# A fused attention and feed-forward kernel: both first maxima and both first exponentials of two units taken at once

## What is computed

```
x = x + tanh(g_xattn) * attention(layernorm(x), ctx)
x = x + tanh(g_ffn)   * ffn(layernorm(x))

attention, per batch and head h:
  scores = q_r[h] @ k_r[h].T          # 512 x 1024, inner size 64
  attn   = softmax(scores)            # row maximum, exponential with row sum, division
  ctx_c  = attn @ kv_rope             # 512 x 128
  out   += ctx_c @ (w_kc_kv[h].T @ Wo[h])
ffn: act_quant(rmsnorm(.)) @ w1, @ w2; silu(a) * b; act_quant(rmsnorm(.)) @ w3
```

## Time and profile before

| | |
|---|---|
| median of 3 runs | 731.63 us |
| the profiled execution, its own time | 732.04 us |
| its span (first to last instruction) | 730.2 us |
| outside the span | 1.84 us |
| busy: PE, DVE, ACT, POOL | 98%, 78%, 67%, 35% |
| PE's granted clock | full speed in all 40 slices |
| pair 7, turns of unit 0 begin | 562.72 us |
| pair 7, turns of unit 2 begin | 596.77 us |

### The profile page before, as it was taken

The page is one execution under the profiler, slowest core; times in us unless marked ns, Lnnn a source line. Parts: engine busy times, 40 slices in busy tenths (PEclk is TensorE's granted clock), DMA queues, the critical chain, the costliest instruction groups (busy, mean ns, idle before and its releaser), DMA issues.

```text
span 730.2 us, 11950 instructions
## 1 busy us (share of the span) xinstructions
PE 715.8 (98%) x4142; PEld 531.6 (73%) x4142; DVE 569.0 (78%) x1016; ACT 487.0 (67%) x821; POOL 252.5 (35%) x235
## 2 busy tenths in 40 slices
PE   9899999999999999999999999999999999999997
PEld 8577788777877787778777877787777676645553
DVE  6778867777787777767878787878887889999873
ACT  3677666666666656666666666666676766478876
POOL 4744422222212222222222222222322334677651
PEclk9999999999999999999999999999999999999999
DMA  7401164114010401040114113543250101000001
GB/s 278 151 31 58 39 236 169 34 39 149 29 57 29 158 29 57 29 158 31 59 58 157 59 59 123 174 153 114 70 188 11 29 1 58 1 1 26 19 30 44
DMA packets 22124, 58.32 MB, mean 80 GB/s; under 512 B 4032, under 2 KB 7232, under 8 KB 21312
## 3 DMA queue, kind: packets, MB, share of 16 engines
q1 hardware_dynamic: 19904, 44.96, 18.3%
q0 software_dynamic: 784, 10.49, 3.8%
q10 hardware_dynamic: 1392, 2.29, 0.9%
HBM read 51.45 MB, written 6.29 MB: 79 GB/s over the span
## 4 chain that ended last, share of the span: by engine, by line
PE 83%; DVE 7%; ACT 3%; POOL 3%; issue 2%; DMA 2%; ACTq 0%; SPq 0%; POOLq 0%; DVEq 0%
PE ps_b L1377 14%; PE ps_s L1324 13%; PE ps_ctx L1335 9%; PE ps_ctx L1337 7%; PE ps_ctx L1336 7%; PE ps_s L587 4%; PE ps_b L1233 4%; PE ps_b L1231 4%; PE ps_b L1232 4%; PE ps_b L1297 2%; PE ps_b L638 2%; PE ps_b L1266 2%; PE ps_b L1299 2%; PE ps_b L1298 2%; PE ps_b L1303 2%
## 5 line engine op out<-in xcount | busy, mean ns | idle before, releaser
L1128 POOL TENSOR_SCALAR E<-E,small 128x1024 f32<-128x1024 f32 x128 | 148.1, 1157 | 415.1 <-DVE small L1680 415.1
L1471 ACT ACTIVATE et_hi<-ps_b 128x512 fp32r<-128x512 f32 x256 | 152.8, 602 | 163.9 <-PE ps_b L1377 163.7
L1636 DVE TENSOR_TENSOR et_lo<-ps_b,et_hi 128x512 fp32r<-128x512 f32 x256 | 175.5, 686 | 54.5 <-ACT et_hi L1471 53.0
L1675 DVE TENSOR_REDUCE small<-ps_s 128x1 f32<-128x1024 f32 x128 | 155.7, 1217 | 4.5 <-PE ps_s L1324 3.0
L1377 PEld LDWEIGHTS ps_b<-ident,E 128*128 128x128 f32 x1024 | 124.7, 140 | 40.1 <-issue 8.8
L1377 PE MATMUL ps_b<-ident,E 128*128 128x128 f32 x1024 | 152.3, 273 | 0.3 <-POOL E L1128 0.3
L1514 ACT ACTIVATE E<-ps_s,small 128x1024 f32<-128x1024 f32 x128 | 142.9, 1117 | 5.7 <-DVE small L1675 5.0
L1335 PE MATMUL ps_ctx<-et_hi,kv_hi 128*128 128x512 f32 x256 | 121.0, 473 | 0.5 <-DVE ctx_lo L1636 0.5
L1337 PE MATMUL ps_ctx<-et_lo,kv_hi 128*128 128x512 f32 x256 | 101.1, 395 | 0.0
L1336 PE MATMUL ps_ctx<-et_hi,kv_lo 128*128 128x512 f32 x256 | 100.5, 393 | 0.0
L1661 DVE SCALAR_TENSOR_TENSOR x_sb<-ps_b,small,x_sb 128x512 f32<-128x512 f32 x62 | 46.3, 746 | 29.1 <-PE ps_b L1233 29.0
(11 more groups left out here) (188 smaller groups left out, 1070.6 us busy)
## 6 DMA issues: line engine op xcount, KB each, us to landing
w_stage<-in_wffn SPq DMA_DIRECT2D x48, 512.0 KB, 3.4
xnT<-xn_split POOLq DMA_DIRECT2D x3, 2048.0 KB, 9.5
wo_s<-in_woT SPq DMA_DIRECT2D x8, 512.0 KB, 6.4
xn_split<-xnT POOLq DMA_DIRECT2D x2, 2048.0 KB, 9.3
wq_s<-in_wq SPq DMA_DIRECT2D x7, 512.0 KB, 6.2
wkcq_s<-in_wkcqT SPq DMA_DIRECT2D x7, 384.0 KB, 4.4
out<-x_sb SPq DMA_DIRECT2D x8, 256.0 KB, 2.0
x_sb<-in_x SPq DMA_DIRECT2D x3, 512.0 KB, 7.0
```

What stands on the lines that cost most here:

```text
L1128: nc.gpsimd.tensor_scalar(e, e, rowinv[:, k:k + 1], 1.0, ALU.mult, ALU.mult).then_inc(scaled, 1)
L1471: return nc.scalar.activation(out, in_, ACT.Copy)
L1636: return nc.vector.tensor_tensor(out, full, hi.bitcast(F32), ALU.subtract)
L1675: nc.vector.tensor_reduce(negmax[:, k:k + 1], ps_s[:, t % 2, :], AX_X, ALU.max, negate=True).then_inc(max_done, 1)
```

## The change

A new function `at_once` is true in units 0 and 2 of pair 7. There, in step 0, DVE takes the maxima of tiles 0 and 1 of the next unit in a row, ahead of the low part of block 0 (before: maximum 0, low part 0, maximum 1). ACT computes exponential 0 and exponential 1 in a row behind the high part of block 0 (before: exponential 0, high part 1, exponential 1). Nothing is added or taken away, and no wait is changed.

```diff
--- before.py
+++ after.py
@@ -61,6 +61,12 @@
 MAX_FIRST = {0: 0}
 MAX_STEP = {0: 1, 3: 2, 4: 3}
 EXP_STEP = {0: 0, 1: 1, 4: 2, 5: 3}
+
+
+def at_once(variant, w):
+
+
+    return variant == "last" and w in (0, 2)
 INV_STEP = {1: 0, 2: 1, 5: 2, 6: 3}
 
 
@@ -1552,7 +1558,10 @@
                     act.wait_ge(et_done, 32 * p + (8 * w + c + 1))
                     copy_act(et_hi[:, c % ET_RING, :], ps_b[:, bank_of(variant, ("turn", w, c)), :]).then_inc(ethi_done, 1)
                     if c in EXP_STEP and not (variant == "last" and w == 3):
-                        exp_tile(act, *next_unit(p, w), EXP_STEP[c])
+                        if not (c == 1 and at_once(variant, w)):
+                            exp_tile(act, *next_unit(p, w), EXP_STEP[c])
+                        if c == 0 and at_once(variant, w):
+                            exp_tile(act, *next_unit(p, w), EXP_STEP[1])
                     if (w, c) == WK_AT and variant != "last":
                         wk_high(act, 16 * p + 32)
                     if (w, c) == KV1_AT and variant == "first":
@@ -1715,6 +1724,8 @@
                         side_low(dve, p, variant, task, ps_b[:, bank_of(variant, task), :])
                     if c in MAX_FIRST and scores:
                         max_tile(dve, *next_unit(p, w), MAX_FIRST[c])
+                        if at_once(variant, w):
+                            max_tile(dve, *next_unit(p, w), MAX_STEP[c])
                     dve.wait_ge(ethi_done, 32 * p + (8 * w + c + 1))
                     lo_part(et_lo[:, c % ET_RING, :], ps_b[:, bank_of(variant, ("turn", w, c)), :], et_hi[:, c % ET_RING, :])\
                         .then_inc(et_split, 1)
@@ -1723,7 +1734,7 @@
                         inv_tile(dve, *next_unit(p, w), INV_STEP[c])
                     if late and c == 5:
                         inv_tile(dve, *next_unit(p, w), 3)
-                    if c in MAX_STEP and scores:
+                    if c in MAX_STEP and scores and not (c in MAX_FIRST and at_once(variant, w)):
                         max_tile(dve, *next_unit(p, w), MAX_STEP[c])
                     if (w, c) == WK_AT and variant != "last":
                         wk_low(dve, p + 2)
```

## The result

The changed kernel takes 733.35 us, the median of 9 runs (732.65 to 734.66), beside 731.79 us before (9 runs, 731.57 to 732.19). The ratio is 1.0020, with a 95% interval of 1.0011 to 1.0028: about 1.5 us slower. The interval leaves out 1, so these runs told a change of this size from none, which the prediction had doubted. The forecast was 732.8, with 732.4 to 733.1 as its likeliest stretch and a range of 731.8 to 733.9: the measured time lies above that stretch and inside the range. The profiled execution takes 733.35 us, with a span of 731.5.

What follows compares the result with a forecast made beforehand. The prediction took PE, busy almost all the time, to bound the kernel. Unit 0's 0.95 us and unit 2's 0.20 us sum to 1.15 us, added to 731.63 for 732.8 us, range 731.8 to 733.9.

Steps and rivals of the forecast that it cites:

- The gain of 0.90 us in each unit: Units 0 and 2: PE's second half of the scores starts 0.90 us earlier, leaving 0.18 us of wait in unit 0.
- High part 1 and low part 1, 0.95 us later, and `ctx_lo` behind them: Unit 0: low part 1 runs 0.95 us later, so `ctx_lo` holds PE's next product but one; cost 0.95 us.
- The delay is carried on in full from unit 0: After unit 0: PE has no wait left there to swallow the delay, so all 0.95 us is carried on.
- Unit 2, 0.33 to 0.41 us, of which 0.20 reach unit 3: Unit 2: the product behind `ctx_lo` starts 0.33 to 0.41 us later; 0.20 us counted as passed on.
- The collision of L849 with POOL is repeated: Unit 0, DVE: L849 again sits out POOL's scale of tile 0, taking 1.03 us ahead of `ctx_lo`.
- the rival of the lost collision: Unit 0: POOL's scale comes over 0.12 us later against L849, `ctx_lo` up to 0.92 us earlier; 731.9 us; 8%.
- The sum, +1.15: Whole kernel: 0.95 us from unit 0 plus 0.20 us from unit 2, giving a median of 732.8 us.
- theory A: Expected of e1: `ctx_lo` holds PE behind high part 1 and low part 1; 0.95 us cost, 732.7 to 732.8 us.
- The rival for "slower by more": Behind unit 2: one more L889 falls under a POOL product, costing 0.82 us more; 733.6 us; 20%.
- my line at 0.2%: Whole kernel: a median above 733.09 us counts as slower by over 0.2%; given 23%.
- The rival that would have been faster: Units 0 and 2: only the wait before the scores counts, `ctx_lo` does not hold PE; 730.7 to 729.8 us; 5%.

Runs made afterwards that it cites:

- e4: The changed kernel with `ctx_lo` on DVE moved ahead of the small feed-forward work in both units; 731.66 us, ratio 0.9996.
- e6: The changed kernel with `ctx_hi` ahead of high part 1 and `ctx_lo` ahead of low part 1 in both units; 731.84 us, ratio 0.9995.
- e7: The changed kernel with reciprocal 0 in unit 0 moved behind the four small DVE instructions; 732.31 us, ratio 1.0004.
- e2: The changed kernel with the change kept in unit 2 alone; 732.00 us, ratio 1.0000 to the kernel before.
- e10: The changed kernel run once more, word for word; 733.33 us, ratio 1.0026 to the kernel before.
- e1: The changed kernel with the change kept in unit 0 alone; 734.46 us, ratio 1.0026 to the kernel before.

## Why the prediction was right

**The gain of 0.90 us in each unit.** Right: PE's wait before the scores fell to 0.18 us in both, as written.

**High part 1 and low part 1, 0.95 us later, and `ctx_lo` behind them.** Right. The step that decided the sign was to ask what the next instruction but one of PE waits for, and to notice that it was just held already: 1.66 us against 1.59 for the same gap. The new wait was put at 1.9 us and is 1.85; the product of unit 0 was put 0.95 us later, and is. e4 and e6 show the cause by taking it away.

**The delay is carried on in full from unit 0.** Right: PE is ready for the second half of unit 2's scores 0.95 us later (601.33 - 0.18 - 0.14 against 601.15 - 1.09), and e7, which takes 0.86 us out of unit 0, shifts the turned rows by 0.80 less.

**Unit 2, 0.33 to 0.41 us, of which 0.20 reach unit 3.** Right: 0.32 and 0.19 (1.14 less 0.95); in e2, alone, 0.23.

**The collision of L849 with POOL is repeated.** Right, and e7 shows what it is: without the overlap 0.17 us, with it 1.02. That fits what the prediction cites of the Trainium skill, page "SBUF — State Buffer", section "SBUF: two separate sides", by which the one that starts first keeps the other out. Only one half of it is seen here, POOL first and DVE held. In e7 POOL's tile comes after the instruction has ended, so no run shows POOL shut out, as the rival of the lost collision had it.

**The sum, +1.15.** The six executions of the change and five of e10 at the full clock have a median of 733.21, 1.2 to 1.4 us above the 731.79 and 731.97 beside them; the traces show 1.14 and 1.17 at the turned rows. At the end of the trace it is about 1.2 us (spans of 731.5 and 730.2, less the 0.14), so the delay stayed to the end, as written. The mechanism and its size held; the median of 733.35 is 0.4 us further above its own kernel before than the forecast. The executions at 0.998 move that median by only 0.1 us (the six others alone have 733.25). The rest, 0.3 us, is gone in e10, whose executions at the full clock lie 1.2 us above those of before, and is no more than what the medians of the kernel before differ by (731.63 to 731.97).

What the prediction left out is the clock. It named an idle wait of 1.9 us on PE, wrote "nothing runs at a fixed time of its own, so I expect the delay to stay", and did not ask what PE's clock does behind such a wait. In 6 of 17 executions of the change that costs 1.3 to 1.4 us more. With fewer than half of the executions low it hardly shows in the median, which is luck: in e1, where six of nine are low, the median is 1.7 us above the 732.7 to 732.8 of theory A. The rival for "slower by more" had another cause, a second collision of L889 with POOL; at 618.47 that instruction took 0.88 us as before, so it did not come. The median crossed my line at 0.2% (733.09), to which I had given 23%, and not for the reason that I had given.

**The rival that would have been faster** fell at its own point: `ctx_lo` ends far behind 567.7.

## What to carry to other kernels

Before giving an operation to an engine earlier, list what it overtakes there, and follow that to whoever waits for it; a wait that is removed from PE is only a gain if the next thing PE waits for is not already as late. Where two chains end within a tenth of a microsecond, shortening one of them buys at most that tenth, and here lengthening the other cost ten times as much. And look at single executions, not at the median alone: on PE a long idle wait can cost a second time, in the clock, in some executions and not in others. Here the remedy that paid was to shorten the wait.

## What the hardware showed that I had not expected

Behind an idle wait of 1.86 us on PE the granted clock fell to half for 3.4 us in one traced execution, at a price of 1.58 us; in the two other traces with that wait (the change and e10) it stayed full. By their mean clock (0.998) and their times, 12 of 26 executions with that wait lost the same, and the others kept the full clock; one program on one chip did both. With 0.99 us or less of waiting for `ctx_lo` there it happened in none of 77 executions, and with the wait filled by transposes in none of 7. The kernel before shows a clock as low in 2 of 79, untraced. Why it comes in one execution and not in the next stays open.
